# Output-weight pieces of head pairs 1, 3 and 5 moved four quarters earlier, those of pair 7 two, in a fused decoder layer

## The reference

```python
def _mxfp4_matmul(x, codes, scales, block_size=BLOCK):
    w = codes * jnp.repeat(scales, block_size, axis=0)
    return x @ w
q, k, v = (each _mxfp4_matmul(x, w_codes, w_scales) + b), reshaped to (B, S, 16, 128)
scores = jnp.einsum('bqhd,bkhd->bhqk', q, k) / jnp.sqrt(jnp.float32(HEAD_DIM))
attn = jax.nn.softmax(scores, axis=-1)
out = jnp.einsum('bhqk,bkhd->bqhd', attn, v).reshape(B, S, NUM_HEADS * HEAD_DIM)
return _mxfp4_matmul(out, wo_codes, wo_scales) + bo
```

## Time and profile before

| | |
|---|---|
| median of 3 runs | 937.73 us (937.46 to 937.91) |
| the profiled execution's own time | 936.67 us |
| its span in the trace | 934.8 us |
| granted TensorE clock over the span | 0.995 of full speed |
| PE busy | 910.9 us, 97% of the span |
| DVE, ACT, POOL busy | 590.4 (63%), 582.3 (62%), 503.7 us (54%) |
| quarters 0 to 127 | about the first 500 us |

### The profile page before, as it was taken

One profiled execution on the slowest core, in us unless ns is written; L12 is line 12 of the kernel. 1 busy time (PEld: TensorE's weight loads), 2 busy tenths in 40 slices (PEclk: granted clock), 3 DMA queues, 4 the chain that ended last, 5 costly groups with the idle time before them and its releaser, 6 DMA issues.

```text
span 934.8 us, 13242 instructions
## 1 busy us (share of the span) xinstructions
PE 910.9 (97%) x4440; PEld 749.5 (80%) x4440; DVE 590.4 (63%) x1056; ACT 582.3 (62%) x1155; POOL 503.7 (54%) x415
## 2 busy tenths in 40 slices
PE   8999999999999999999989999899999999999997
PEld 7788788887788877887768788788888888888885
DVE  5666966678666776667584799976698125411114
ACT  4667876687767778787876576444654635433333
POOL 4257652646616467377765467644674752354440
PEclk9999999999999999999999999999999999999999
DMA  7532230122300322213112212332433341343321
GB/s 204 158 95 64 75 101 1 49 71 74 102 1 29 91 61 79 65 57 86 50 57 90 78 36 91 90 102 72 129 105 112 102 124 34 115 129 92 94 80 45
DMA packets 46103, 76.97 MB, mean 82 GB/s; under 512 B 5585, under 2 KB 11217, under 8 KB 45777
## 3 DMA queue, kind: packets, MB, share of 16 engines
q1 hardware_dynamic: 45600, 75.68, 27.8%
q10 hardware_dynamic: 432, 0.39, 0.2%
HBM read 73.69 MB, written 2.36 MB: 81 GB/s over the span
## 4 chain that ended last, share of the span: by engine, by line
PE 39%; DVE 9%; ACT 2%; issue 1%; POOL 1%; ACTq 0%; DVEq 0%; POOLq 0%
PE p L917 6%; PE p L921 6%; PE p L918 6%; PE p L931 3%; PE p L933 3%; PE p L932 3%; DVE m L1605 3%; DVE SX L1613 1%; DVE SCL L1613 1%; PE p L879 1%; PE p L880 1%; PE p L884 1%; DVE st L1565 1%; PE p L894 1%; PE p L730 1%
## 5 line engine op out<-in xcount | busy, mean ns | idle before, releaser
L1532 DVE TENSOR_SCALAR_CACHE_REDUCE JK<-p,ssc 128x512 bf16<-128x512 f32 x112 | 83.7, 747 | 113.6 <-PE p L677 113.6
L2032 POOL TENSOR_TENSOR V<-RAW,V 128x512 fp32r<-128x512 f32 x64 | 82.5, 1310 | 132.5 <-ACT V L1099 132.5
L1042 ACT ACTIVATE PR<-p,nms,ssc 128x512 f32<-128x512 f32 x112 | 87.4, 781 | 61.6 <-DVE JK L1532 60.2
L2028 POOL TENSOR_TENSOR acc<-SX,acc 128x512 f32<-128x512 f32 x58 | 75.0, 1293 | 84.3 <-ACT SX L1079 51.7
L695 PE MATMUL p<-R 128*128 128x512 f32 x248 | 97.2, 392 | 0.8 <-DVE V L1525 0.8
L1545 DVE TENSOR_TENSOR PT<-p,PT 128x512 fp32r<-128x512 f32 x128 | 87.4, 683 | 5.2 <-ACT PT L1061 5.1
L2032 POOL TENSOR_TENSOR C<-RAW,C 128x512 fp32r<-128x512 f32 x58 | 76.7, 1335 | 25.5 <-ACT C L1099 25.5
L1853 DVE TENSOR_TENSOR SX<-p,SX 128x512 f32<-128x512 f32 x32 | 22.1, 690 | 101.4 <-PE p L921 91.6
L730 PEld LDWEIGHTS p<-ident,PR 128*128 128x128 f32 x512 | 62.6, 140 | 21.3 <-DVE PT L1545 6.6
L730 PE MATMUL p<-ident,PR 128*128 128x128 f32 x512 | 77.8, 274 | 1.0
L1061 ACT ACTIVATE PT<-p 128x512 fp32r<-128x512 f32 x128 | 75.7, 591 | 0.0
(11 more groups left out here) (249 smaller groups left out, 2727.7 us busy)
## 6 DMA issues: line engine op xcount, KB each, us to landing
RAW<-in_wg SPq DMA_DIRECT2D x32, 256.0 KB, 2.9
RAW<-in_wu SPq DMA_DIRECT2D x32, 256.0 KB, 2.6
RAW<-in_ctxn SPq DMA_DIRECT2D x32, 256.0 KB, 2.8
RAW<-in_wd SPq DMA_DIRECT2D x32, 256.0 KB, 2.8
RAW<-in_wq SPq DMA_DIRECT2D x19, 256.0 KB, 2.7
RAW<-in_wk SPq DMA_DIRECT2D x18, 256.0 KB, 2.7
RAW<-in_wv SPq DMA_DIRECT2D x16, 256.0 KB, 2.9
RAW<-in_wo SPq DMA_DIRECT2D x16, 256.0 KB, 4.5
```

What stands on the lines that cost most here:

```text
L1042: e.activation(PR[:, i % 2, :], P[i % 2][:, :], ACT.Exp, bias=nms[:, i % 4:i % 4 + 1], scale=ssc[:, 0:1] if HB[j][0] > 1 else SC, accum_ou ...
L1532: e.tensor_scalar(JK[:, :], P[i % 2][:, :], ssc[:, 1:2] if HB[i // 4][0] > 1 else -SC, None, ALU.mult, ALU.min, accum_out=nms[:, i % 4:i % ...
L2028: e.tensor_tensor(acc[:, r], scaled_at(4 * q + tt), acc[:, r], ALU.add).then_inc(*rows[r].up((q, 1)))
L2032: e.tensor_tensor(lo, RAW[:, slot[key], :], hi, ALU.subtract).then_inc(*c_lo.up(key))
```

## The change

`pieces_at` takes the quarters of the output pieces from a list, where a formula gave them before. All else in the program is as it was; what the other engines do follows from `pieces_at`.

```diff
+OPIECES = (2, 3, 14, 15, 34, 35, 46, 47, 66, 67, 78, 79, 98, 99, 104, 105)
+
 def pieces_at(i):
     j, qt = divmod(i, 4)
@@
-    if qt >= 2 and (j % 4 == 0 and j < 28 or j == 26):
-        out.append(("o", (j // 2 if j < 24 else j - 12) + qt - 2, 0))
+    if i in OPIECES:
+        out.append(("o", OPIECES.index(i), 0))
     return out
```

## The result

| | before | after |
|---|---|---|
| median of 20 runs each | 937.65 us (936.35 to 940.45) | 939.41 us (937.56 to 943.40) |
| ratio after to before, with its 95% interval | | 1.0021 (1.0014 to 1.0028) |
| the profiled execution's own time | 936.67 us | 939.80 us |
| span | 934.8 us | 938.0 us |
| granted TensorE clock over the span | 0.995 | 0.992 |

A forecast was written before the change was run, and what follows sets the result against it. PE, busy 910.9 of 934.8 us, bounds the kernel, so only its waits count. Pairs 1, 3, 5 and 7 give 1.3 + 0.5 + 0.5 - 1.05 = 1.2 us on 937.73: 938.9 us, range 936.3 to 941.2.

The forecast's parts named there:

- quarter 16: `value_bias` and coefficients: Pair 1: 1.5 us for `value_bias` without idle DVE time, 0.4 for tiny instructions beside busy POOL; bounds 0.7 and 2.8.
- pair 7: removed, added, net: Waits in quarters 110 and 112 go, -1.6 us; two more ACT instructions before `attend` of 108, +0.55; sum -1.05.
- What is removed: Less ACT and DVE work ends waits near quarters 24, 56, 88 (-3.3 us together) and in 110, 112 (-1.6).
- Rivals 1 and 4: Additions covered, removals real: 935.3 us, chance 0.11; nothing visible, vanished waits come back elsewhere: 937.7 us, chance 0.12.
- Slots and DMAs: Moved pieces' loads cost 0: SP issues them several quarters ahead of `multiply`, and slots come free no later than before.
- rival 3: A moved piece waits for its slot or load, pair 7 closest: 1 us or so, 939.9 us; chance 0.06.
- DVE at quarters 48 and 80: Second `value_bias` beside POOL's `low` delays `maximum` of 51; PE loses 1.06 us per pair; bounds 0.3 and 1.3.
- ACT's term: Two `look` between `exponential` and `pt_high` of 51 make `attend` wait 0.5 us; bounds 0.3 and 0.65.
- the lower bound of 0.3: Smallest `attend` wait from the two `look` at quarter 51, since the 5.77 us holds about 0.2 of idle ACT.
- Pair 1: Quarters 16 to 24: 1.9 us at DVE, 0.5 for two `look`, 1.1 back; net +1.3 us.
- Rival 2: DVE held longer at quarter 16: 941.8 us with about 2 us of half clock, 939.8 without; chance 0.13, half with clock.
- the sign that the prediction had named for being wrong: A granted clock below full near quarter 18, listed among what would show the forecast wrong.

The follow-up runs named there:

- e6: Changed kernel with POOL's `low` of heads 3, 7 and 11 one quarter later, and the `look` that follows: 936.65 us, ratio to before 0.9985.
- e5: Changed kernel with `value_bias` of heads 3, 7 and 11 left out: 935.64 us, ratio to before 0.9974.
- the second set of runs: The whole change, unaltered, run and profiled once more against the kernel before: 939.18 us, ratio 1.0016.
- e7: Changed kernel with `coefficients` moved from quarter 16 to 31, their two tiny `exp` on ACT to 28: 936.97 us, ratio to before 0.9983.
- f3: Kernel before, without the change, with `coefficients` in quarter 31 and their ACT part in 28: 937.68 us, ratio to before 0.9993.

## Why the prediction was right, and where it was not

The time forecast was 938.9 us, the same within 0.2%, and the median is 939.41. The mechanism held at every place, but the closeness of the number owes something to two errors of opposite sign.

| term | forecast, us | measured |
|---|---|---|
| pairs 1, 3, 5: waits removed | -1.1 each | all gone |
| `value_bias` in 48 and 80 | +1.06 | `maximum` 1.05 later (4.03 for 4.04); PE 0.88 + 0.15 |
| two `look` ahead of `attend` | +0.5 | 0.25, and 0.1 on its first matmul |
| pairs 3 and 5, net | +0.5 each | +0.35, +0.33 |
| quarter 16: `value_bias` and coefficients | +1.9 | 1.54 at the scores |
| pair 1, net | +1.3 | +0.84 |
| pair 7: removed, added, net | -1.6, +0.55, -1.05 | gone; +0.47 (and 0.1); -0.88 |
| sum of the waits | **+1.2** | **+0.64** |
| half clock behind quarter 18 | 0 in the sum | 1.2 us in about 0.7 of the executions (estimate), +0.85 |

- **What is removed** was right: ACT's `look` and `high` were the cause, and nothing took their place at quarters 24, 56, 88, 110 and 112. Rivals 1 and 4 fall with this: the additions were not covered, and the waits did not come back.
- **Slots and DMAs** were put at 0, and the cost was 0, but not for the reason given. The sign of rival 3 came, and for the pair it had named: POOL waited 2.71 us for the load of pair 7's second piece, which SP could not issue several quarters ahead. The multiply had time to spare there, so the price was 0 and not 1 us.
- **DVE at quarters 48 and 80** was right to 0.01 us at `maximum` and to 0.03 at PE (1.03 for 1.06), because quarter 36 was the right analog. It was right for the reason given, that POOL's `low` has just been released by the `high`: e6 took that away and the `value_bias` fell to 0.74. The Trainium skill, GPSIMD Engine Reference, section 1 (Specifications), says that POOL contends with VectorE instructions with two SBUF inputs; the rows agree, and e5 shows that the instruction's size doesn't matter: 0.22 us alone and 1.33 beside POOL for 128x1.
- **ACT's term** was too large by 0.25. The distance from `exponential` of 51 to `attend` of 52 is 225.75 - 220.25 = 5.50 us, not the 5.77 taken from pair 7, which held about 0.2 us of idle ACT; the lower bound of 0.3 had named that. At pair 7's own new place the figure was nearly exact: 0.47 for 0.55.
- **Pair 1** was too large by 0.36 at DVE. `value_bias` took 1.22 us from start to next start, not the 1.5 of quarter 36, since POOL's instruction beside it was nearer to its end; the coefficients took 1.40 us, 0.33 more than before, where 0.4 was added.
- **The clock** is the step that failed: the sum has nothing for it. Rival 2 had it, at the right place, but tied it to `exponential` of 19 coming 2.8 us later; a wait that was 1.54 us longer, 2.0 in all, was followed by the half clock in three of four profiles, which is the sign that the prediction had named for being wrong. Its price was put at 2 us and is 1.2, and it got half of 0.13, where it belonged in the sum with about 0.85 us. The trace of before has full clock behind waits of about 1 us and half clock behind the one of 2.3; between these it shows nothing, and a forecast of 2.4 us of wait (0.47 and 1.9) should not have been taken as free.
- **Same or slower.** Had the terms been exact, the forecast would have been 937.73 + 0.64 + 0.85 = 939.2, still the same side of 0.2%, but nearer to the edge; the second set of runs gives 1.0016. The measured ratio of 1.0021 lies on that edge.

One thing is only partly settled. Against their sums of waits (with 0.85 for the clock where it applies) all variants are within their intervals, but e7 (-0.8 by the profile, -1.6 by the ratio) and e5 (-1.9 and -2.4) lie low, and the first set of runs of the change lies high (1.5 and 2.0). Intervals of 1.1 us to either side for the first two don't tell that from chance.

## What to carry to other kernels

Before moving an instruction of DVE with two SBUF inputs, look at what POOL has queued at that moment, and count about the rest of POOL's instruction on top of its own time, whatever its size (0.83 us more for a rest of 1.03 in quarter 48, 1.11 for 1.31 in e5); the same work two quarters earlier, or POOL's a quarter later, cost 0.2 us or less here. Where a change lengthens a wait of PE to about 2 us, put the half clock into the sum with a share of the executions, and compare several executions before reading a difference of two profiles. Look for small foreign work in the crowded stretch too: moving six tiny instructions out of quarter 16 turned the same change from a loss into a gain. And look beyond the engine that bounds the kernel: POOL's new wait of 2.7 us was longer than any new one of PE and cost nothing.

## What the runs showed of the hardware that was not expected

- A DVE instruction on 128x1 with two SBUF inputs took 0.22 us with POOL idle and 0.55, 0.89 and 1.33 us beside a POOL instruction, each time until that one had ended. The TENSOR_SCALAR and RECIPROCAL instructions next to it took 0.14 to 0.21 in all of them.
- It holds the other way too: with DVE's `value_bias` waiting, POOL's following instruction took 1.73 us where it otherwise takes 1.28.
- The same wait of 2.0 us left the clock at full speed in one execution and was followed by about 3.5 us at half speed in three others, with the same instructions around it.
- The half-clock stretch behind quarter 122 lasted about 3.5 or about 7 us, in changed and unchanged kernels alike, which makes a difference of 0.85 us; the start of the program varied by 2 us between profiles; and a stretch of the same length cost nothing at 602 to 612 us and 1.5 us at 617 (e6, f3). Two profiles of one and the same kernel can therefore lie as far apart as this change's whole effect.
